# Making W_down's parts during the first two chunks' lists, after the first chunk's norm

## The reference

```python
q = (x @ Wq + bq).reshape(B, S, N_HEADS, D_QUERY)
s1 = jnp.einsum('bshd,nd->bshn', q1, K1)      # q2, K2 likewise
v1, i1 = jax.lax.top_k(s1, TOPK)              # s2 likewise
all_scores = (v1[..., :, None] + v2[..., None, :]).reshape(..., TOPK * TOPK)
vals, best = jax.lax.top_k(all_scores, TOPK)
scores = jax.nn.softmax(vals, axis=-1)
h = jnp.einsum('bsd,bshkd->bshk', x, W_down[expert_idx])
h = jax.nn.gelu(h, approximate=False) * scores
out = jnp.einsum('bshk,bshkd->bsd', h, W_up[expert_idx])
```

## Time and profile before

| | us |
|---|---|
| median of 3 runs | 3705.01 |
| lowest and highest | 3697.02 and 3714.77 |
| the profiled execution, its own time | 3710.8 |
| its span in the profile | 3709.0 |
| what lies around the span | 1.8 |
| granted TensorE clock, mean over the span | 0.882 |

### The profile page before, as it was taken

The page is one execution under the profiler, slowest core; times in us unless marked ns, Lnnn a source line. Parts: engine busy times, 40 slices in busy tenths (PEclk is TensorE's granted clock), DMA queues, the critical chain, the costliest instruction groups (busy, mean ns, idle before and its releaser), DMA issues. The chain is left out here.

```text
span 3709.0 us, 90949 instructions
## 1 busy us (share of the span) xinstructions
PE 3227.4 (87%) x31732; PEld 2785.6 (75%) x31732; DVE 3194.2 (86%) x15276; ACT 2119.9 (57%) x4379; POOL 1343.9 (36%) x990
## 2 busy tenths in 40 slices
PE   5999999933598999988999899998999889999988
PEld 3666666612588888888888888888888788888887
DVE  4566666536999999999999999999999999999981
ACT  3444444413566666666666666666666666666662
POOL 1333333331143343333434334443334333443353
PEclk9999999965698999988888888888888888998888
DMA  2121111131133333322333333322323333333332
GB/s 61 46 62 52 52 52 52 40 154 71 66 112 109 104 103 112 101 101 101 118 112 113 109 115 113 112 101 101 115 101 101 101 104 115 121 115 112 109 115 95
DMA packets 132324, 356.85 MB, mean 96 GB/s; under 512 B 13866, under 2 KB 61610, under 8 KB 129453
## 3 DMA queue, kind: packets, MB, share of 16 engines
q1 hardware_dynamic: 131868, 351.03, 28.1%
HBM read 309.01 MB, written 25.17 MB: 90 GB/s over the span
## 5 line engine op out<-in xcount | busy, mean ns | idle before, releaser
L999 POOL TENSOR_TENSOR b_hid<-b_hid,b_gates 128x512 f32<-128x512 f32 x512 | 760.8, 1487 | 909.6 <-ACT b_hid L1255 909.1
L1124 PE MATMUL b_ps_a<-b_wup,b_hid 128*128 128x256 f32 x4096 | 955.7, 379 | 0.0
L1113 PE MATMUL b_ps_h<-b_xT_hi,b_wd_split 128*128 128x256 f32 x4096 | 929.2, 312 | 14.4 <-ACT b_hid L1255 10.1
L1124 PEld LDWEIGHTS b_ps_a<-b_wup,b_hid 128*128 128x128 f32 x4096 | 743.6, 190 | 84.0
L1113 PEld LDWEIGHTS b_ps_h<-b_xT_hi,b_wd_split 128*128 128x128 f32 x4096 | 707.5, 202 | 28.6 <-issue 19.0
L1040 PE MATMUL b_ps_s<-b_ohr,b_ohq 80*128 80x32 f16 x16384 | 447.0, 183 | 239.4 <-issue 239.1
L1234 ACT ACTIVATE b_ohq<-b_q_no,b_minus_qid 80x128 f16<-80x128 f16 x2048 | 648.1, 390 | 1.0
L1040 PEld LDWEIGHTS b_ps_s<-b_ohr,b_ohq 80*128 80x128 f16 x16384 | 438.1, 101 | 246.7 <-issue 245.9
L1113 PE MATMUL b_ps_h<-b_xT_lo,b_wd_split 128*128 128x256 f32 x2048 | 600.4, 293 | 0.0
L1159 ACT ACTIVATE b_gates<-b_ps_s 128x512 f32<-128x512 f32 x512 | 305.8, 597 | 384.6 <-PE b_ps_s L1040 377.4
L1255 ACT ACTIVATE b_hid<-b_ps_h 128x512 f32<-128x512 f32 x512 | 303.0, 592 | 291.1 <-PE b_ps_h L1113 291.1
(11 more groups left out here) (186 smaller groups left out, 5317.0 us busy)
## 6 DMA issues: line engine op xcount, KB each, us to landing
b_wd_split<-wd_parts SPq DMA_DIRECT2D x512, 512.0 KB, 3.5
a_keysh<-a_key SPq DMA_DIRECT2D x16, 896.0 KB, 5.4
a_x<-in_x SPq DMA_DIRECT2D x16, 512.0 KB, 4.9
x_between<-a_y SPq DMA_DIRECT2D x16, 512.0 KB, 3.2
b_x<-x_between SPq DMA_DIRECT2D x32, 256.0 KB, 2.7
wd_parts<-b_wd_split SPq DMA_DIRECT2D x16, 512.0 KB, 3.1
b_x1t<-x_between SPq DMA_DIRECT2D x32, 256.0 KB, 4.2
out<-b_y SPq DMA_DIRECT2D x32, 256.0 KB, 2.3
```

The source lines that it names most:

```text
L999: G.tensor_tensor(hid[:, p % 4, :, :], hid[:, p % 4, :, :], gates[:, 2 * p:2 * p + 2, :], ALU.mult).then_inc(mix_done, 1)
L1113: mm = T.matmul(hbank[p % 2][:, j * C:(j + 1) * C], a, c, start=i == 0, stop=i == len(parts) - 1)
L1124: mm = T.matmul(abank[:, t * D:(t + 1) * D], hid[:, p % 4, j, t * P:(t + 1) * P], wup[:, 2 * p + j, :], start=p == 0 and j == 0 and t == 0 ...
```

## The change

W_down's load keeps its place on SP, W_up's goes behind the stores. The making of the parts goes into the loops: on ACT parts 0 to 7 at the head of turn -2 and 8 to 15 at the head of turn -1; on POOL in the same turns behind `root` (and, if there were any, the `mix` steps) and ahead of `low_x`; on SP the stores of parts 0 to 7 at the end of turn -3 and of 8 to 15 at the end of turn -2, each time after the load of a chunk, and after the second half come W_up's load and the wait for all stores. What is computed is the same.

```diff
@@ sp_program
-        def keep_parts():
+        def load_wdown():
             sp.dma_start(wdown, w["wdown"].rearrange("(k p) r q -> p k r q", p=P)).then_inc(wdown_in, 16)
-            sp.dma_start(wup[:, :, :], w["wup"]).then_inc(wup_in, 16)
-            for p in range(PAIRS_R):
+
+        def keep_parts(half):
+            for p in range(half * PAIRS_R // 2, (half + 1) * PAIRS_R // 2):
                 sp.wait_ge(wd_lo_done, p + 1)
                 sp.dma_start(wd_dram[p], whole_slot(p)).then_inc(wd_out[p % WD_SLOTS], 16)
+
+        def parts_kept():
+            sp.dma_start(wup[:, :, :], w["wup"]).then_inc(wup_in, 16)
             for i in range(WD_SLOTS):
                 sp.wait_ge(wd_out[i], 16 * len(range(i, PAIRS_R, WD_SLOTS)))
...
         load(0)
-        keep_parts()
+        load_wdown()
         for m in range(-3, chunks + 1):
...
             if has(m + 4):
                 load(m + 4)
+            if m in (-3, -2):
+                keep_parts(m + 3)
+            if m == -2:
+                parts_kept()
@@ pool_program
-        for p in range(PAIRS_R):
-            low_down(p)
         for m in range(-3, chunks + 1):
             if has(m + 3):
                 root(0, m + 3)
             for p in range(PAIRS_R):
                 if has(m):
                     mix(m, p)
+
+            if m in (-2, -1):
+                for p in range((m + 2) * PAIRS_R // 2, (m + 3) * PAIRS_R // 2):
+                    low_down(p)
             if has(m + 3):
                 low_x(m + 3)
@@ act_program
-        for p in range(PAIRS_R):
-            high_down(p)
         for m in range(-3, chunks + 1):
+            if m in (-2, -1):
+                for p in range((m + 2) * PAIRS_R // 2, (m + 3) * PAIRS_R // 2):
+                    high_down(p)
             for p in range(PAIRS_R):
```

## The result

The changed kernel took 3669.86 us at the median (3668.5 to 3673.35, 4 runs), the kernel before it 3703.72 (3697.02 to 3714.77, 4 runs). The ratio is 0.9906, with a 95% interval of 0.9889 to 0.9923: faster, by 34 us. The forecast was 3668.9, a ratio of 0.990 to the 3705.01 of three runs; the fourth run brought the median before to 3703.72.

The account below looks back on a forecast made before the run. DVE's list of work was taken to set the pace, PE close behind, so an earlier start moves everything: 36.6 us removed less 0.5 for POOL beside DVE is 36.1, from 3705.0 to 3668.9 us, range 3657 to 3683.

Parts of the forecast that it names:

- The part removed: Fill, chunk 0: POOL's root no longer stands behind 16 `low_down`, so it starts at 808.35, not 844.91: 36.6 us earlier.
- Norm to lists: Fill, chunk 0's norm to its first list: PE, ACT and DVE take the same durations, lists start at 821.8.
- The bound of 3.2 us for the clock: First queries on PE: TensorE's clock may differ, by half of the 16 queries' 6.47 us in either direction.
- Chunk 1's load: Turn -3, SP: load behind W_down lands by 819.7, variance ends 820.7, before lists at 821.8; cost nothing, 1.1 us cover.
- two of DVE's waits: DVE in the fill: only 37.7 us for POOL's root and 7.2 us at chunk 0's decode are of note.
- ACT held by eight parts: Turns -2 and -1: eight copies hold ACT 9.6 us, 16.5 with slow stores; cost nothing, 4.3 us left before PE's sum of picks.
- What POOL costs DVE: Turns -2 and -1: POOL's subtractions beside DVE lengthen the gates' product by 0.5 us, bounds 0 and 4.4; lists unaffected.
- The sum: Whole kernel: 36.6 - 0.5 = 36.1 us gained, 3668.9 against 3705.0, 1.0% less; chance 0.84.
- The first: Parts late in turn -1, or chunk 1's load in turn -3, beyond 18.4 us cover: 3672 to 3682; chance 0.07.
- The second: POOL blocks DVE: each of 16 subtractions holds a list instruction 1.27 us, 20.3 us lost, 3688.7; chance 0.04.
- The third: Chunks fall otherwise to TensorE's clock, more become 88.6 us long; slower, 3734 if all 29 are long; chance 0.03.
- The fourth: Norm goes first, yet a load or ACT starts the lists where they were: 3705; chance 0.02.

Follow-up runs that it names:

- Experiment 1: Kernel before, with only chunk 0's root put ahead of POOL's 16 subtractions, ACT's copies left ahead: median 3699.54 us, ratio 0.9984, fill 181.95 us.
- Experiment 2: Changed kernel with parts 0 to 7 again made ahead of the loops on ACT, POOL and SP: median 3694.75 us, ratio 0.9969, fill 171.41 us.
- experiment 4: Changed kernel with all 16 parts made in turn -2 instead of eight in each of two turns: median 3668.38 us, ratio 0.9896.
- experiment 3: Changed kernel with W_up's load again right behind W_down's: median 3679.02 us, ratio 0.9931, fill 158.19 us.
- experiment 6: Changed kernel with POOL's eight subtractions of a turn started only after DVE's norm of that turn: median 3665.43 us, ratio 0.9895.
- experiment 7: Changed kernel with each of POOL's subtractions of turn -1 done four times over: median 3677.18 us, ratio 0.9921, fill 158.88 us.

## Why the prediction was right

- **The part removed.** 36.6 us forecast, 36.57 measured from the variance to the norm. Experiment 1 adds what the text only implied: POOL's order alone is worth 3.3 us, and ACT's had to go with it. Experiment 2 shows that the gain is not in proportion to the parts moved: half of them gave 13.8 of the 32.9 us, since one part ahead of the norm is enough to bring the wait for W_down.
- **Norm to lists.** The same durations were taken, and 0.13 us more came. The bound of 3.2 us for the clock was sound: this stretch was 11.0 us in experiment 4 and 12.6 in the changed kernel.
- **Chunk 1's load.** Landing at 819.7 at the latest was the bound, 1.1 us of cover. It landed at about 816.0, and the variance ended 2.1 us before the lists could start. The cover is real but thin: experiment 3 takes it away, at 5.9 us. The prediction called two of DVE's waits the only ones of note; the same list has 7.0 us for two chunks' loads and 6.5 for ACT's scores, and the loads are what experiment 3 brought out.
- **ACT held by eight parts.** 9.6 us forecast for turn -1. It was 9.2, from 878.35 to 887.55 (10.0 in turn -2), stores landing 2.9 us after issue at the median. The queries' end kept 7.3 us of cover where I had 4.3, partly since DVE itself was later.
- **What POOL costs DVE.** This term was mis-sized: 0.5 us taken, 2.65 measured (0.83 + 1.00 + 1.89 - 1.07), inside the bounds of 0 and 4.4. The step that failed is the one that took the norm's median of 404 ns for its length beside a busy POOL. In the kernel before, only 22 of the 64 halves of norms overlap a product of POOL's at all. In 21 of these DVE's came first, by 0.2 us or more, and kept its 0.40 us, while the product behind it took up to 1.35 us for a median of 1.28. The one that came second, 0.22 us into a product, is the one of 1373 ns, and it ended 0.15 us after the product. Beside subtractions that follow one another without a gap DVE comes second nearly always: in turn -1 the gates' product and both halves of the norm did. The maximum of 1373 ns was the value to take for work placed side by side.
- **The sum.** 36.1 forecast, 32.9 in the fill; the rest is that term, 0.9 of clock at the decode and 0.1 ahead of the lists. The median came out at 3669.86 against 3668.9. That it is so near is in part luck: the fill gave 3.2 us less than forecast, and the scatter of the long chunks gave some of it back. Beside their own runs of the kernel before, the changed kernel's medians were 33.9, 34.7 and 32.6 us lower. Two figures of the prediction do not follow from its own terms: 10 us beyond the cover make 3679 and not 3682, and 9, 3.2 and 3.9 us upward make 3685 and not 3683.
- **Rivals.** The first did not occur and needs more than experiment 6 or 7 gave it: ACT's delay of 16 us more in experiment 7 moved the first down product only by what DVE lost. The second, a whole subtraction for each, is refuted by the lists of experiment 7. The third is refuted in its mechanism: long chunks keep their numbers while the start of the chunks moves by up to 39 us (decode 1 at 993.48 before, at 953.98 in experiment 6), and their stops stand where a packet of PE's instructions is late, not where the clock is low. The fourth, something else that holds the lists where they were, did not occur; with POOL's order alone, in experiment 1, it did, and the something was ACT.

## What to carry to other kernels

A long wait in the fill of a pipeline is worth only what the next engine in the chain leaves of it: here the same order stood in two programs, and changing POOL's alone gave 3 us of 33. When setup work is moved under running work, move its transfers behind the small loads of the critical chain too (6 us here), and look at what it meets on the engine that sets the pace; for that read the maximum of a row, not its median, and look which of the two engines came first. Beside lists of MAX8 and its like, some 40 us of POOL's subtractions cost DVE nothing.

## What the runs showed of the hardware that was not expected

Two things held an engine here that no semaphore of the program stands for, though the description of the cores above says that only semaphores do.

A DVE norm or conversion, or a sum or product of two tiles, of 0.2 to 0.4 us that begins behind one of POOL's subtractions or products lasts until 0.03 to 0.19 us after the end of that one, up to 1.4 us in all. The subtractions stay at 1.26 to 1.39 us (4.06 us for three), so beside a chain of them it was DVE that waited nearly every time. Where DVE came first, its norm kept 0.40 us. In the profiles before and after and of experiments 4, 6 and 7, some 13,000 MAX8, FIND_INDEX8 and MATCH_REPLACE8 began inside such an instruction of POOL's, and none took over 0.24 us.

PE stopped for 2.1 to 3.3 us in the middle of a run of small products, at the same product of the same chunks in kernels whose starts and instruction counts differ, without a wait that the profile names. Each such stop stands at the same place of a group of 256 of PE's instructions and ends 1.2 to 1.6 us after a packet of 16 KB on the queue that carries instructions. The stops make the chunks of 86 to 88.7 us and cost 11 to 24 us of an execution.
